# Scores of a narrow-headed attention as one f16 product over stacked high and low parts, instead of an f32 product over masked queries

## The reference, cut to what matters

```python
HEADS, DK = 16, 8
q = layernorm(x) @ Wq.T            # 8 batches, 256 x 128
k = ctx_768 @ Wk.T
v = ctx_768 @ Wv.T
q, k, v = (t.reshape(B, T, HEADS, DK).transpose(0, 2, 1, 3) for t in (q, k, v))
attn = softmax(einsum('bhqd,bhkd->bhqk', q, k) * DK ** -0.5)
x = x + einsum('bhqk,bhkd->bhqd', attn, v).transpose(0, 2, 1, 3).reshape(B, 256, 128) @ Wo.T
```

## Time and profile before

| | |
|---|---|
| time, median of 3 runs | 1691.09 us (1690.98 to 1693.81) |
| profiled execution, its own time | 1687.73 us |
| its span | 1686.0 us |
| busy over the span | PE 83%, DVE 68%, ACT 48%, POOL 26% |
| second layer's attention (583 to 893 us) | PE busy 256.3 of 310 us, DVE 232.0, ACT 179.8, POOL 105.2; granted clock 0.90 |
| a stretch within it (752 to 786 us) | PE 30.9 of 34 us, DVE 27.7, ACT 21.8, POOL 12.7; granted clock 0.95 |

### The profile page before, as it was taken

How to read it: one execution, slowest core, us unless ns; L and a number is a source line. 1 busy time by engine, 2 the same in 40 slices (tenths; PEclk the granted TensorE clock), 3 DMA queues, 4 the chain that set the end, 5 groups by cost and what they waited for, 6 DMA issues and landing times.

```text
span 1686.0 us, 38925 instructions
## 1 busy us (share of the span) xinstructions
PE 1397.7 (83%) x12511; PEld 1079.4 (64%) x12511; DVE 1145.0 (68%) x3358; ACT 815.7 (48%) x1792; POOL 431.0 (26%) x753
## 2 busy tenths in 40 slices
PE   4899999978999979998966746688849899898977
PEld 2577777765666658777755625566636677776654
DVE  4788888876766668888865437643338877787861
ACT  1666666654333346666642222322217655566642
POOL 2000000011111223433322367533241322222321
PEclk7999999989999989999978967699959999999999
DMA  8999000000000210000001100131100000000000
GB/s 228 283 113 112 0 0 0 0 1 1 1 1 0 67 49 5 3 3 6 4 4 43 36 25 20 52 97 41 55 25 2 2 0 0 0 0 0 0 2 25
DMA packets 109761, 55.08 MB, mean 33 GB/s; under 512 B 44593, under 2 KB 102578, under 8 KB 109474
## 3 DMA queue, kind: packets, MB, share of 16 engines
q1 hardware_dynamic: 106146, 46.53, 14.6%
q0 software_dynamic: 3520, 7.31, 1.3%
HBM read 27.09 MB, written 26.74 MB: 32 GB/s over the span
## 4 chain that ended last, share of the span: by engine, by line
PE 54%; DVE 21%; issue 10%; POOL 5%; ACT 4%; SPq 2%; DMA 1%; POOLq 1%; DVEq 1%; ACTq 0%
PE bank L1610 46%; PE bank L1614 8%; DVE PTs L2376 4%; DVE negm L2362 2%; DVE Pm L2356 2%; DVE VxF L797 2%; DVE negm L2365 2%; ACT Pm L1446 1%; SPq L893 1%; ACT PTs L1400 1%; POOL token_rows_by_expert L1123 1%; DVE st L2146 1%; POOLq L665 1%; POOL yn L1334 1%; DVE OT L2136 1%
## 5 line engine op out<-in xcount | busy, mean ns | idle before, releaser
L1446 ACT ACTIVATE Pm<-bank,negm 128x256 f32<-128x256 f32 x528 | 221.2, 471 | 214.4 <-DVE negm L2365 123.3
L1610 PE MATMUL bank<-kT,Qz 64*128 64x256 f32 (+2 forms) x1568 | 307.4, 411 | 15.8 <-ACT Pm L1446 6.4
L1614 PE MATMUL bank<-ident,Pm 128*128 128x128 f32 x1568 | 237.1, 286 | 63.9 <-DVE PTs L2376 59.9
L2376 DVE TENSOR_TENSOR PTs<-bank,PTs 128x512 f16<-128x512 f32 x384 | 251.3, 682 | 40.4 <-ACT PTs L1400 39.7
L1614 PEld LDWEIGHTS bank<-ident,Pm 128*128 128x128 f32 x1568 | 178.9, 145 | 141.1 <-issue 96.9
L1610 PEld LDWEIGHTS bank<-kT,Qz 64*128 64x128 f32 (+1 forms) x1568 | 188.6, 193 | 96.2 <-issue 54.1
L1400 ACT ACTIVATE PTs<-bank 128x512 f16<-128x512 f32 (+1 forms) x388 | 215.8, 591 | 3.4 <-PE bank L1614 3.3
L1610 PEld LDWEIGHTS bank<-VxF,PTs 128*128 128x128 f16 (+1 forms) x4672 | 186.1, 101 | 11.9 <-DVE PTs L2376 3.4
L1610 PE MATMUL bank<-VxF,PTs 128*128 128x65 f16 (+3 forms) x4672 | 190.2, 189 | 2.5 <-DVE PTs L2376 2.3
L1446 ACT ACTIVATE Pm<-Pm,negm 128x256 f32<-128x256 f32 x256 | 109.7, 497 | 117.1 <-DVE negm L2356 89.9
L2365 DVE TENSOR_REDUCE negm<-bank 128x2 f32<-128x512 f32 x136 | 93.6, 688 | 40.3 <-PE bank L1610 37.0
(11 more groups left out here) (317 smaller groups left out, 2184.1 us busy)
## 6 DMA issues: line engine op xcount, KB each, us to landing
token_rows_by_expert<-trash SPq DMA_DIRECT2D x10, 1782.0 KB, 17.8
Qz<-token_rows_by_expert SPq DMA_DIRECT2D x62, 66.0 KB, 1.8
Qz<-expert_rows_by_token SPq DMA_DIRECT2D x12, 256.0 KB, 3.1
R<-in_L_ffn_ew SPq DMA_DIRECT2D x2, 1024.0 KB, 7.1
R<-in_L_ffn_w SPq DMA_DIRECT2D x1, 2048.0 KB, 9.5
R<-in_L_xattn_Wkv SPq DMA_DIRECT2D x2, 768.0 KB, 6.4
R<-in_L_ffn_w SPq DMA_DIRECT2D x1, 1408.0 KB, 11.9
R<-in_L_xattn_Wq SPq DMA_DIRECT2D x2, 512.0 KB, 3.9
```

What stands on the lines that cost most here:

```text
L1446: last = act.activation(masked, masked if A.mask == "full" else bank[k % 2][:, qt * S:(qt + 1) * S], ACT.Exp, bias=negm[:, k % 4, qt:qt + ...
L1610: return pe.matmul(o, l, r, start=start, stop=stop)
L1614: return pe.transpose(o, i, ident[0:n, 0:n])
L2376: dve.tensor_tensor(PTl[:, k % 4, :], bank[2 + k % 2][:, :], PTh[:, k % 4, :], ALU.subtract).then_inc(s.pt[1].sem, 1)
```

## The change

Scores come from f16. A fill of q or k leaves the bank as a high part (ACT rounds the scaled value) and a low part (DVE: scaled value less high), each 128 x 512. The factors come from bounds that the set-up finds (`headscale`); their inverse product, times the softmax scale, is applied behind the scores. SP writes both parts to DRAM and reads them back in bands of 24 rows: head h = 4j + g lies in rows 32g to 32g+23 of column block j, for k as (high, high, low), for q as (high, low, high). One f16 product over these 24 rows is q high by k high, q low by k high and q high by k low. The bands of k lie where kT was and in R0, those of q in `Qz`. The masks and `headmask` go. The row maxima take two DVE operations, the exps a second pointer operand. The fills q 0 to 2 move into the last chunk of the feed-forward, which is written out by itself; the G of the first feed-forward moves from `Qz` to R0. PE's loop over the batches in the middle is written out.

```diff
+NEXT_QUERIES = {(3, 0): ("q", 0), (4, 0): ("q", 1), (5, 0): ("q", 2)}
...
                 st.append(("up", (e, ft)))
...
+                if F.n == 0 and final and (e, ft) in NEXT_QUERIES:
+                    st.append(("context", NEXT_QUERIES[e, ft]))
...
+        G = {0: cols(R0, 0, 2048).rearrange("p (g s) -> p g s", s=CH),
+             3: Qz[:, :, :].rearrange("p h s -> p (h s)").rearrange("p (g s) -> p g s", s=CH)}
+        bandsq = Qz[:, :, :].rearrange("p h s -> p (h s)").bitcast(F16).rearrange("p (j t) -> p j t", t=T)
+        bandsk = [t.bitcast(F16).rearrange("p (j t) -> p j t", t=T)
+                  for t in (kT[:, :, :].rearrange("p h s -> p (h s)"), cols(R0, 9472, 2048))]
...
+            if A.n == 1 and eng is nc.tensor:
+                for b in range(1, B - 1):
+                    body(b, "mid")
...
+            with eng.Fori(1, last - (F.n == 0 and last == NCH)) as c:
                 body(c, False)
+            if F.n == 0 and last == NCH:
+                body(NCH - 1, False)
...
+            def head_rows_written(kind, c):
...
+                sp.dma_start(head_rows[kind][:, :, c * CH:(c + 1) * CH], head_parts(kind, c)).then_inc(head_rows_out[kind], 16)
+            def in_bands(dst, kind, js, ts, done):
+                src = head_rows[kind].rearrange("(j g d) u t -> u g d j t", j=4, g=4, d=8)
+                for g in range(4):
+                    for i, u in enumerate((0, 0, 1) if kind == "k" else (0, 1, 0)):
+                        sp.dma_start(dst[32 * g + 8 * i:32 * g + 8 * i + 8, :, ts], src[u][g][:, js, ts]).then_inc(done, 16)
+            for c in range(NCH):
+                head_rows_written("k", c)
+            sp.wait_ge(head_rows_out["k"], 16 * NCH)
+            in_bands(bandsk[0], "k", slice(0, 2), slice(0, T), key_bands[0])
+            for c in range(3):
+                head_rows_written("q", c)
+                sp.wait_ge(head_rows_out["q"], 16 * (c + 1))
+                in_bands(bandsq, "q", slice(0, 4), slice(c * CH, (c + 1) * CH), query_bands[0])
             need(sp, ffn_s[0].y, NCH * FFN[0].E)
+            in_bands(bandsk[1], "k", slice(2, 4), slice(0, T), key_bands[1])
             load("b2", b2all, a["L1_ffn_b2"].rearrange("(o e) d -> o (e d)", o=1).to_broadcast([P, 8 * D]))
...
+            head_rows_written("q", 3)
+            sp.wait_ge(head_rows_out["q"], 16 * 4)
+            in_bands(bandsq, "q", slice(0, 4), slice(3 * CH, T), query_bands[1])
...
-            pool.partition_all_reduce(vmaxall[:, 0:3], vmax[:, 0:3], P, RMAX).then_inc(setup_vmaxall, 1)
+            pool.partition_all_reduce(vmaxall[:, 0:6], vmax[:, 0:6], P, RMAX).then_inc(setup_vmaxall, 1)
...
+                        for rows in xr[2:4]:
+                            link(pool.memset(rows[:, :, :, D + 1:ROW], 0.0))
...
-                        masks(None, 0, (0, 4))
                         last_rows()
-                        masks(None, 0, (8, 12))
...
-                    if A.n == 1 and kinds == "first":
...
-                        masks(0, 1)
-                    if A.n == 1 and kinds == "mid":
-                        masks(b, b + 1, (0, 4))
                     if A.n < 2 and kinds == "first":
                         largest(A.n)
...
+                            factor = headscale[:, 2:3] if A.n == 1 else -1.0 if A.mask == "full" else 1.0
...
-                                                      scale=-1.0 if A.mask == "full" else 1.0)
+                                                      scale=factor)
...
+                            move(head_parts(kind, k)[:, 0, :], bank_of(m)[:, :], headscale[:, w:w + 1]).then_inc(s.headhigh.sem, 1)
...
+                            if A.n == 1 and kinds == "first" and k in (0, 8):
+                                pe.wait_ge(key_bands[k // 8], 16 * 12)
+                                if k == 0:
+                                    pe.wait_ge(query_bands[0], 16 * 36)
+                            if A.n == 1 and kinds == "mid" and b == 1 and k == 0:
+                                pe.wait_ge(query_bands[1], 16 * 12)
...
-                                last = mm(o, Qz[:, k, qt * P:(qt + 1) * P], keys_of(A, b, k))
+                                if A.n == 1:
+                                    rows, j = slice(32 * (k % 4), 32 * (k % 4) + 24), k // 4
+                                    last = mm(o, bandsq[rows, j, b * S + qt * P:b * S + (qt + 1) * P],
+                                              bandsk[j // 2][rows, j % 2, b * S:(b + 1) * S])
...
+                dve.tensor_reduce(vmax[:, 4:5], w1nat[:, 0:128], AX.X, ALU.max, apply_absolute_value=True)
+                dve.tensor_reduce(vmax[:, 5:6], w1nat[:, 128:224], AX.X, ALU.max, apply_absolute_value=True)
...
+            def head_scales(A):
+                q, k, both = (headscale[:, i:i + 1] for i in range(3))
+                dve.tensor_scalar(q, vmaxall[:, 4:5], P / 2.0 ** 13, 2.0 ** -60, ALU.mult, ALU.max)
+                link(dve.tensor_scalar(k, vmaxall[:, 5:6], vmaxall[:, 0:1], DC / 2.0 ** 13, ALU.mult, ALU.mult))
+                link(dve.tensor_scalar(k, k, 2.0 ** -60, None, ALU.max))
+                link(dve.tensor_scalar(both, k, q, A.scale, ALU.mult, ALU.mult))
+                dve.reciprocal(headscale[:, 0:2], headscale[:, 0:2]).then_inc(head_scale_set, 1)
...
+                                chain(dve.tensor_reduce(rowmax[:, k % 4, :], v, AX.X, ALU.max, negate=True))
+                                dve.tensor_scalar(nm, rowmax[:, k % 4, :], headscale[:, 2:3], None,
+                                                  ALU.mult).then_inc(s.negmax.sem, 1)
...
+                            if (kind, k) == ("k", 0):
+                                head_scales(A)
...
+                            dve.scalar_tensor_tensor(low, bank_of(m)[:, :], headscale[:, w:w + 1], high,
+                                                     ALU.mult, ALU.subtract).then_inc((s.ring.dve if m % 2 else s.headlow).sem, 1)
```

## The result

The changed kernel takes **1702.5 us** (median of 4 runs, 1701.98 to 1705.67) against 1691.3 for the kernel before on the same chip: 1.0063 times, 95% interval 1.0048 to 1.0078. It is slower by 0.6%, clear of the interval; 1670.3 was forecast, 1687 was the upper end of the range.

A forecast was written before the change was run, and what follows sets the result against it. TensorE was taken to bound plain heads at 1.70 us, with DVE and ACT as slow after the change; gains between heads. Terms sum to -20.8 us, from 1691.09 to 1670.3 us; range 1654 to 1687.

The forecast's parts named there:

- the one that set the change of rows at nothing: Second layer's scores: switching TensorE between 24 and 128 rows, twice a head, was taken to cost almost nothing.
- the third rival: Second layer's attention: PE stays the bound at the low clock, paying two row changes a head; 1708 us, chance 0.11.
- rows 13: First layer's 424 transpose records with 2.5 us of idle time before them, cited against any cost of changing rows.
- The clock: Second layer's attention: with less to do PE may be granted 1.2 GHz throughout; 1.56 us a head, by itself no bound.
- Ring: Plain heads: DVE reduction, ACT exps and copy, DVE low and norm set the pace; 3.39 us for two heads.
- small operation: Plain heads: DVE's dependent operation behind each row-maximum reduction, taken to add 0.20 us for two heads.
- the second pointer of the exps: ACT's exps with two pointer operands: 0.18 us more for two heads; rival that it is overlapped, 1659 to 1662, chance 0.13.
- Between heads: Middle batch: DVE work around residual, choice and ranks that plain heads can't hide, 1.43, 1.48 and 1.14 us.
- the -12.0: Five middle batches of the second layer's attention: 31.2 us each for 33.56, together 12.0 us saved.
- Batch 0: First batch of the stage: all-reduce no longer waits for masks, 8.7 us back; less 1.2 for maxima, -7.0 in all.
- `rk`: End of the rank steps: 1.89 us, read as waiting for a POOL mask, would fall to its neighbours' 0.17.
- Start: Start of the stage: q's bands must land before the first scores, first reduction at 588.0 for 584.63, +3.4 us.

The follow-up runs named there:

- 128 rows: Changed kernel with its f16 score products over all 128 rows, other heads' rows cleared, in place of 24 rows: 1682.7 us (0.9949 of the kernel before).
- immediate factor: Kernel over 128 rows with constant scales, DVE's small operation put back between reduction and exps as a product by one: 1673.8 us (0.9878).

## Why the prediction was wrong

**The step that failed is the one that set the change of rows at nothing.** It was the third rival that came, at 1702.5 of its 1692 to 1724, with a chance of 0.11. Its two halves were both seen and each set aside by itself: of the low clock the prediction says "By itself this is no bound", and against the changes it holds "the idle time of rows 13". Together they make the bound. At 1.2 GHz PE needs 0.85 for four transposes, 0.37 for av and 0.38 for the scores, 1.60 us; the changes add 0.28; 1.88 is above the 1.72 that DVE and ACT allow. Over 128 rows 1.60 stays below it, and the low clock is not seen in the time. That the changes at the full clock would stay below it too is an estimate (some 1.0 + 2 x 0.09) that no run tried. The rival's size is in part luck: it had 1.98 a head and 4.7 us a batch between heads, where 1.88 and 6.2 came, and so 36.4 a batch for 36.3.

**The row was misread.** Idle time ahead of a product counts from the modelled end of the product before, and such a record goes on long after its columns have streamed: transposes 0.21 apart have records of 0.42. A pause of 0.1 to 0.13 lies within the record and shows as no idle time. It shows in the distance from start to start, and the kernel before had it: in the first layer, a fill on 96 rows and the scores on 64 behind it,

```profile
202.20 0.59 PE L1610 MATMUL bank<-R,ctxb 96*128 96x512 f32 x1
202.72 1.13 PE L1610 MATMUL bank<-kT,Qz 64*128 64x256 f32 x8
```

are 0.52 apart, where two such fill products are 0.43 apart; the scores' last product and the transposes behind it are 0.306 apart for 0.216. So a change cost 0.09 at the full clock in the very rows that were cited for zero. The Trainium skill, page TensorEngine Tiling (Array Packing), section Key Properties, had it right that a change of tiling mode drains the engine; the page gives no figure, and the runs here put it at 0.09 a change at 2.4 GHz and at 0.28 for a head's two changes at 1.2.

**The clock was half foreseen.** The rival took it from PE having less to do. The runs show that only over 128 rows, where twice the products raised the clock from 0.71 to 0.88. On fewer rows something else holds: all seven kernels with score products on a part of the rows (24, 32 or 64, f16 or f32, single to fourfold) were granted 0.50 between 620 and 820 us, up to PE busy all the time, and all seven over 128 rows 0.71 to 0.94. In the changed kernel the clock fell behind PE's wait of 4.85 us for the first exps and came back only with the next feed-forward. The kernel before also fell at its first scores, behind a wait of 1.91, to 0.67 in the 5 us from 582 on, and had 0.99 in the 7 us after them, where the changed one had 0.50. Rows and changes were not tried apart, since each narrow product here stands between wide ones. But fourfold products leave the number of changes as it was and do not move the clock.

**Ring: right.** 3.39 for two heads was forecast; 128 rows give 3.45 (1.51 + 1.94), and the chain in the rows is the one that was forecast. In that kernel:

```profile
693.01 0.68 DVE L2437 TENSOR_REDUCE rowmax<-bank 128x2 f32<-128x512 f32 x1
693.72 0.23 DVE L2438 TENSOR_SCALAR negm<-rowmax,headscale 128x2 f32<-128x2 f32 x1
693.86 0.68 DVE L2452 TENSOR_TENSOR PTs<-bank,PTs 128x512 f16<-128x512 f32 x1
694.46 0.68 DVE L2437 TENSOR_REDUCE rowmax<-bank 128x2 f32<-128x512 f32 x1
694.90 0.59 ACT L1443 ACTIVATE PTs<-bank 128x512 f16<-128x512 f32 x1
695.17 0.23 DVE L2438 TENSOR_SCALAR negm<-rowmax,headscale 128x2 f32<-128x2 f32 x1
695.52 0.69 DVE L2452 TENSOR_TENSOR PTs<-bank,PTs 128x512 f16<-128x512 f32 x1
...
696.45 0.68 DVE L2437 TENSOR_REDUCE rowmax<-bank 128x2 f32<-128x512 f32 x1
```

ACT's copy ends at 695.49 and the low starts at 695.52, 2.51 behind the reduction at 693.01 (forecast 2.08 + 0.20 + 0.18 = 2.46); low and norm add 0.93. DVE's own work is close below: its first low starts 0.14 behind the small operation, the second 0.35, so 0.2 of the 3.44 is that wait and 3.24 is DVE's (forecast 3.15). 32 of the stage's 128 lows wait for ACT like this.

The small operation is worth 2.1/8 = 0.26 for two heads (forecast 0.20). The other 1.6/8 = 0.20 is not the second pointer of the exps alone: up to 0.12 of it can be the small operation's own pointer. The exps went from 472 to 560 ns, as foreseen. That their pointer is not overlapped rests on the ring's rows (with an immediate factor such a low comes 2.27 behind its reduction, not 2.51); no run tried it by itself.

**Between heads: too small.** Even over 128 rows a middle batch takes 33.4, not 31.2: the heads with the residual, the choice and the ranks cost 1.8, 1.8 and 1.2 above a plain one and the rest together 1.0, which is 5.8 against the forecast's 4.1. Of the -12.0 that kernel has -0.5: this is the second term that failed, and why 128 rows come to 1682.7 and not to 1670.3. What it gains is batch 0 (-5.5), the start (-1.2), batch 1 (-1.5) and little else.

**Batch 0 and `rk`: right in the mechanism.** Both waits went as forecast. No wait ahead of `upback` (before: 8.73), and `rk` takes 0.16 (before: 1.89):

```profile
617.21 0.14 DVE L2403 TENSOR_SCALAR upback<-uprowall 128x1 f32<-128x1 f32 x1
```

```profile
762.25 0.16 DVE L2597 TENSOR_TENSOR rk<-ohacc 128x8 f32<-128x8 bf16 x1
```

Batch 0 gave 5.3 of the 7.0 all the same: its heads beside a maximum cost 0.26 each (forecast 0.2), and head 4, with the fill of `q` 3 behind it, took 7.20 for 6.22. And what `rk` gave back in a middle batch (head 14: 2.94 for 4.28) went into plain heads (0.18 each) and fills at the low clock (head 4: 2.41 for 1.90; 7: 3.97 for 3.09; 12: 3.94 for 2.93).

**Start: wrong sign.** -1.3 for +3.4. An issue of the bands takes 0.34, not 0.55, and q0 is written at 553.2, not 558.5, so the three rounds end ahead of the feed-forward. The first two heads' scores run at 580.12 and wait for DVE, which ends the feed-forward first:

```profile
553.22 0.54 SPq L988 DMA_DIRECT2D head_rows_q<-xnT  x1
555.67 4.06 SPq L995 DMA_DIRECT2D Qz<-head_rows_q  x12
...
568.87 4.29 SPq L995 DMA_DIRECT2D Qz<-head_rows_q  x12
```

## What to carry to other kernels

Read a suspected pause of TensorE from the distance between the starts of its records, not from idle time: modelled ends hide what is shorter than a record. Before a product is cut to few rows, add up PE's chain at the low clock, with each change of rows in it; here the same f16 products over cleared full rows were 20 us faster than over 24 rows. And two causes that are harmless one by one belong in one sum: the low clock alone fits under the pace of DVE and ACT (1.60 of 1.72 us), the changes alone should, and together they did not.

## What was not expected of the hardware

Score products on 24, 32 and 64 of 128 rows went with a granted clock of 0.50 for 300 us and more, at any load that was tried; the first layer's products on 64 rows, which run in pairs on the two halves, went with 1.00 between 60 and 340 us. And giving PE each score product twice over 128 rows raised its clock from 0.71 to 0.88 at no cost in time (1682.7 and 1683.2 us).
